# Heads layer of a graph network: ScalarE copies the turned edge pairs behind both heads' masked scores, and TensorE turns the maxima and the result ahead of the pairs' scores

## The reference

```python
h_edge = ((atom[src] + bond) @ W).reshape(-1, H, D)      # H = 2, D = 64
el = einsum('ehd,hd->eh', h_edge, attn_l);  er = einsum('nhd,hd->nh', h_node, attn_r)
s = el + er[dst];  s = where(s > 0, s, 0.2 * s)
smax = segment_max(s, dst)
ex = exp(s - smax[dst]);  denom = segment_sum(ex, dst)
ft = segment_sum(h_edge * (ex / denom[dst])[..., None], dst)
h = ft.mean(axis=1)                                       # mean over the heads
```

## Time and profile before

| | |
|---|---|
| median of 3 runs | 8708.57 us (8706.44 to 8710.73) |
| the profiled execution | 8706.0 us, span 8704.2 us |
| heads layer, from its first unit's rows to its last | 113.7 to 2222.2 us, 104 units |
| mean granted clock of TensorE over the span | 0.551 |
| busy over the span | PE 55%, PEld 50%, DVE 78%, ACT 53%, POOL 73% |

### The profile page before, as it was taken

The page is one execution under the profiler, slowest core; times in us unless marked ns, Lnnn a source line. Parts: engine busy times, 40 slices in busy tenths (PEclk is TensorE's granted clock), DMA queues, the critical chain, the costliest instruction groups (busy, mean ns, idle before and its releaser), DMA issues. The chain is left out here.

```text
span 8704.2 us, 123660 instructions
## 1 busy us (share of the span) xinstructions
PE 4760.5 (55%) x23534; PEld 4318.7 (50%) x23534; DVE 6778.0 (78%) x12835; ACT 4571.9 (53%) x12350; POOL 6313.6 (73%) x6672
## 2 busy tenths in 40 slices
PE   5777777777545555555555555555554444444444
PEld 5666666666444444444444444444444444444444
DVE  6888888888577777777777777777777777777777
ACT  5777777777444444444444444444444444444444
POOL 4777777777077777777767777777776777777776
PEclk8666666666655555555555555555555555555555
DMA  2222222222122222222212222222221222222221
GB/s 75 58 58 56 59 58 56 59 58 56 62 32 32 32 32 32 32 32 32 32 30 32 32 32 32 32 32 32 32 32 31 35 35 35 35 35 35 35 35 33
DMA packets 575997, 348.39 MB, mean 40 GB/s; under 512 B 451469, under 2 KB 452365, under 8 KB 575951
## 3 DMA queue, kind: packets, MB, share of 16 engines
q0 software_dynamic: 212992, 229.61, 16.5%
q1 hardware_dynamic: 362239, 118.14, 5.9%
q10 hardware_dynamic: 720, 0.17, 0.0%
HBM read 319.61 MB, written 27.76 MB: 40 GB/s over the span
## 5 line engine op out<-in xcount | busy, mean ns | idle before, releaser
L1620 POOL DMA_INDIRECT plain_rows_in<-table,plain_idx x4992 | 4713.0, 944 | 1775.9 <-issue 1775.9
L1883 PE MATMUL plain_ps_sums<-plain_rows_in,plain_prob 128*128 x10080 | 2349.7, 418 | 0.0
L1883 PEld LDWEIGHTS plain_ps_sums<-plain_rows_in,plain_prob 128*128 128x128 f32 x10080 | 2228.8, 330 | 52.8
L1033 POOL DMA_INDIRECT heads_rows_in<-h_in,heads_idx x1664 | 1589.8, 955 | 588.2 <-issue 507.3
L1904 PE MATMUL plain_ps_max<-ident,plain_column_max 128*128 128x128 f32 x312 | 148.1, 475 | 2375.2 <-DVE plain_column_max L1737 2375.2
L1808 ACT ACTIVATE plain_ps_score<-plain_mask,plain_rows_in 128x128 f32<-128x128 f32 x3744 | 1134.1, 352 | 422.4 <-DMA plain_rows_in<-table,plain_idx 422.4
L1837 ACT ACTIVATE plain_prob<-plain_prob 128x512 f32<-128x512 f32 x936 | 712.3, 772 | 1144.5 <-DVE plain_prob L1756 1134.9
L1904 PEld LDWEIGHTS plain_ps_max<-ident,plain_column_max 128*128 128x128 f32 x312 | 56.9, 182 | 2467.0 <-DVE plain_column_max L1737 2467.0
L1808 ACT ACTIVATE plain_score_sb<-plain_mask,plain_rows_in 128x128 f32<-128x128 f32 x1248 | 398.3, 389 | 1557.0 <-DMA plain_rows_in<-table,plain_idx 1557.0
L1728 DVE TENSOR_TENSOR plain_top<-plain_score_sb,plain_ps_score 128x512 f32<-128x512 f32 x312 | 214.4, 687 | 983.5 <-ACT plain_ps_score L1808 983.0
L1756 DVE TENSOR_TENSOR plain_prob<-plain_prob,plain_ps_max 128x512 f32<-128x512 f32 x936 | 754.0, 861 | 19.9
(11 more groups left out here) (251 smaller groups left out, 8650.5 us busy)
## 6 DMA issues: line engine op xcount, KB each, us to landing
plain_rows_in<-table,plain_idx POOLq DMA_INDIRECT x4992
heads_edges<-in_edge_attr SPq DMA_DIRECT2D x108, 512.0 KB
heads_rows_in<-h_in,heads_idx POOLq DMA_INDIRECT x1664
plain_own<-table SPq DMA_DIRECT2D x324, 33.5 KB
table<-plain_out_sb SPq DMA_DIRECT2D x208, 33.5 KB
plain_dst_ids<-in_dst SPq DMA_DIRECT2D x324, 8.0 KB
plain_unit_par<-unit_floats SPq DMA_DIRECT2D x324, 1.0 KB
plain_unit_int<-unit_ints SPq DMA_DIRECT2D x324, 0.0 KB
```

The source lines that it names most:

```text
L1033: gp.indirect_dma_start(rows_in[h][:, t, :], None, table[:, :], bass.IndirectOffsetOnAxis(ap=idx[h][:, t:t + 1], axis=0)).then_inc(gathere ...
L1620: gp.indirect_dma_start(rows_in[h][:, t, :], None, table[:, :], bass.IndirectOffsetOnAxis(ap=idx[h][:, t:t + 1], axis=0)).then_inc(gathere ...
L1883: ins = te.matmul(sums[h % 2], prob[h % 2][:, t, :], rows, start=t == 0, stop=t == Q - 1)
```

## The change

ACT does `make_masked(n, 1)` directly after `make_masked(n, 0)` and only then `copy_pairs(n + 1)`. Behind `make_mask` the order was `copy_onehot` of chunks 2 and 3, `copy_scores`, `carry_sums`, `copy_result`; it becomes `carry_sums`, `copy_result`, `copy_scores`, `copy_onehot` of chunks 2 and 3. On PE, `score_pairs` and chunks 2 and 3 of `turn_onehot` move from ahead of the turned maxima to behind `turn_result`, which is ahead of the wait for `split_made` and the expansion. No instruction is added or removed; DVE, POOL and SP are as before.

```diff
                         make_masked(n, 0)
+                        make_masked(n, 1)
                         copy_pairs(n + 1)
-                        make_masked(n, 1)
                         copy_onehot(n + 1, after(h), range(0, TURN_BANKS))
                         ac.wait_ge(masked_made, 2 * heads * n + 2 * heads)
                         make_mask(n + 1, after(h))
-                        copy_onehot(n + 1, after(h), range(TURN_BANKS, CHUNKS))
-                        copy_scores(n + 1)
                         carry_sums(n, h)
                         copy_result(n)
+                        copy_scores(n + 1)
+                        copy_onehot(n + 1, after(h), range(TURN_BANKS, CHUNKS))
                         copy_out(i, h, n)
...
                         turn_onehot(n + 1, after(h), range(0, TURN_BANKS))
-                        score_pairs(n + 1)
-                        turn_onehot(n + 1, after(h), range(TURN_BANKS, CHUNKS))
                         te.wait_ge(columns_maxed, heads * n + heads)
                         for hd in range(heads):
                             ins = te.transpose(ps_edge[0:NB, MAX_AT + hd * P:MAX_AT + (hd + 1) * P],
                                                column_max[:, hd, :], con.ident[:, :])
                         ins.then_inc(maxima_turned, 1)
                         turn_result(n, h)
+                        score_pairs(n + 1)
+                        turn_onehot(n + 1, after(h), range(TURN_BANKS, CHUNKS))
 
                         te.wait_ge(split_made, n + 1)
```

## The result

The changed kernel takes 8809.35 us (median of 4 runs, 8804.37 to 8812.64) where the kernel before takes 8707.51: a ratio of 1.012, interval 1.0107 to 1.0132. It is slower by 102 us; the forecast was 8827 us, 118 us over the median before. The profiled span is 8802.6 us, 98.4 us longer, and all of that is in the heads layer.

What follows compares the result with a forecast made beforehand. It took an ACT-DVE-PE ring, 20.47 us a unit, to bound the heads layer. 0.8 x 163 us lost less 0.2 x 63 us won gave +118 us, 8827 us, range 8750 to 8885.

Steps and rivals of the forecast that it cites:

- The new bound: Heads layer, L1153: DVE, which never waited there, waits 2.18 us for PE at the slow clock; forecast's own case, chance 0.81.
- PE's way: PE from turned maxima to expansion: 7.31 us at the slow clock, 4.93 us at 2.4 GHz; DVE wants it at 5.13.
- The row of 3.42 us: Pair scores on PE: 16 instructions take 3.42 us at the level of 0.50, 0.213 us each.
- The 107 ns of the Trainium skill: Pair scores on PE: loads total 1.71 us for 16; gain and loss cancel, 8700 us; rival, chance 0.05.
- The gain on ScalarE: Head 1's masked scores ahead of the pairs' copy: turned maxima 0.56 us earlier, 0.76 in one unit of four; 63 us.
- The sum: Heads layer: +1.62 us a slow unit, -0.56 a fast one; 130 - 13 = +118 us in all.
- The share of the slow level: PE's clock behind the turned result: low in four units of five, 0.8, by judgement.
- The idle time ahead of the first turns: PE between `aggregate` and the first one-hot chunks: some 6 us idle, since the pairs' copy comes later.
- Costed at nothing: Rest of ScalarE's order and `aggregate`: no cost; a late tail was a rival, about +190 us, 8898 us, chance 0.07.
- POOL: POOL's gathers in the heads layer: would wait for ring buffers at some point, at no cost.

Runs made afterwards that it cites:

- e3b: Changed kernel with one of the eight pair-score matmuls, seven left out; 19.18 us a unit on a late-instruction chip, where the changed kernel takes 21.39.
- e4: Changed kernel with the eight pair-score matmuls done twice; units of 24.79 us (slow clock) and 21.71 us (fast), ratio 0.991 on a late-instruction chip.
- e2: Changed kernel with ScalarE's copy of the pairs put back between the heads; 22.05 us a unit against the changed kernel's 21.39, ratio 0.978 on a late-instruction chip.
- e5b: Changed kernel with 14 unused TensorE transposes a unit, held until ScalarE is halfway through head 1; 18.93 us in both units, ratio 0.9979 on a late-instruction chip.
- e5: Changed kernel with 24 unused TensorE transposes a unit at the front of its idle time; 8820.48 us, ratio 1.0109 to the kernel before.
- e5c: Second run of the changed kernel with 14 unused, held-back transposes a unit; 18.93 and 18.99 us in two units, ratio 1.0023 on a late-instruction chip.
- e6: Changed kernel with the second half of one-hot turns behind the projection and sums ahead of the next pairs' turns; units 21.31 and 20.77 us, ratio 0.9914, late-instruction chip.

## Why the prediction was right

- *The new bound.* "DVE waits at L1153 for PE": shown, 80 waits of 2.05 us. e3b takes it away by shortening PE's way, e4 lengthens it instruction by instruction.
- *PE's way.* Forecast 7.31 us at the slow level, measured 7.21. Forecast 4.93 us at the fast one; there L1153 doesn't wait, and the expansion's last instruction ends 1265.42 + 0.36 - 1261.12 = 4.66 us behind the start of the turned maxima. The row of 3.42 us for 16 instructions with 4 columns each was the one that mattered, and it held to 0.01 us. The 107 ns of the Trainium skill (TensorE: Matmul & The Clock Gate, "LDWEIGHTS (loading the stationary operand)") would have given no change; the trace has double that for these fp32 instructions at 0.50.
- *The gain on ScalarE.* Forecast 0.56 us; e2 measures 0.66, and from the start of the masked scores to the turned maxima a unit takes 1261.12 - 1248.43 = 12.69 us, 0.55 less than before (1233.05 - 1219.81). In the 24 fast units the period typically fell by 0.78 inside a round: the turned maxima come mostly 0.65 us earlier, and from there to L1153 are 5.02 us instead of 5.13. The turned maxima themselves took 0.69 us in all 24; where they go at the fast level (0.44 us, e5b), the unit is shorter by another 0.25 us, 18.93 instead of e3b's 19.18.
- *The sum.* +1.62 us became +1.49, -0.56 became -0.78. Both errors point to less loss: forecast 118 us, measured 102.
- *The share of the slow level.* Taken as 0.8 by judgement, measured 80 of 104, 0.77. That it was so near is luck as much as reading. The idle time ahead of the first turns came out as forecast, 621.0 us in 104 times, 6.0 us each, but the level doesn't simply fall with more idle time, as e5's bands show. That the level decides is shown (the 80 and 24 units, the four of e5b and e5c); what sets it stays open.
- *Costed at nothing.* ScalarE's tail and `aggregate` cost nothing, as forecast: no new wait of DVE in `finish` and none of PE behind the expansion. The one-head layers go at the same pace (L1673, first to last start: 8668.7 - 2400.4 before, 8767.1 - 2499.6 after, within 1 us).
- *POOL.* It was held 37.4 us in 16 times in the layer, at no cost, as forecast: DVE waited for gathered rows once, 12.5 us at the start, as before (12.8). What the trace names as the releaser is the load of the indices and not DVE.

## What to carry to other kernels

Before work is moved from an engine's idle time to another place in its queue, measure two things there: how long the engine idles in the new place and how early its next result is ready (1.39 and 1.40 us here), and what the moved work takes at the clock of that place, not at the mean one. And if an order is changed for one engine, follow what stands behind each new wait in the other's queue: e6 took 1.8 us off DVE's wait for PE and found 1.2 to 1.7 of them again behind ScalarE.

## What the runs showed of the hardware

- An fp32 load with a matmul of 4 columns takes about as long as one with 128. Until the next work could start, the 16 of the pair scores took 3.28 us (1240.71 to 1243.99) and the 8 transposes behind them 1.74 us (1243.99 to 1245.73), 0.21 and 0.22 us each at the granted 0.50. At 1.00 the sixteen took 1.85 us instead of 3.41.
- On four of the five chips of the experiments TensorE stood still while the gathers ran, in gaps of about 2 us between single matmuls with no wait to see, and the kernel before took 11,616 to 11,979 us instead of 8708. Durations of single instructions were the same (L1085 1.22 us, the pair scores 3.41). An order that loses 1.2% on the one kind of chip wins 1.4% on the other.
- TensorE's level doesn't simply follow the idle time ahead. 3.25 us of work with hardly a gap behind it was followed by fast pair scores in four units of four (e5b, e5c); 2.78 us of work was followed by 3.41 us of pair scores behind 3.54 us of idle time and by 1.98 us behind 4.88 (e5).
